# Cross-attention block: context rows laid out with their ones columns and loaded whole, and a new order on all five engines

## The reference, cut to what matters

```
n  = layernorm(x)
gi = concat([n, ctx, ctx])                 # q, k and v: q = n, k = v = ctx
ig, fg = gi @ igate_w.T + igate_b, gi @ fgate_w.T + fgate_b
cs = cumsum(log_sigmoid(fg))               # along the 256 rows, per head
log_D = tril(cs[s] - cs[t]) + ig[t];  m = max_t log_D;  D = exp(log_D - m)
C  = (q @ k.T / 8) * D
h  = (C / (max(|sum C|, exp(-m)) + 1e-6)) @ v
x  = x + headnorm(h) * out_w
z  = e4m3(layernorm(x) / s_in);  w = e4m3(ffn_kernel / s_k)
out = x + bf16(z @ w * s_in * s_k) + bias
```

## Time and profile before

| | |
|---|---|
| median of 3 runs | 1749.72 us (1747.93 to 1753.19) |
| span of the profiled execution | 1755.2 us |
| busy in it: PE, DVE | 1600.4 us (91%), 1550.3 us (88%) |
| ACT, POOL | 1284.9 us (73%), 1103.1 us (63%) |
| share of the chain that ended last | PE 61%, DVE 19%, issue 10%, DMA 7% |

### The profile page before, as it was taken

One profiled execution on the slowest core, in us unless ns is written; L12 is line 12 of the kernel. 1 busy time (PEld: TensorE's weight loads), 2 busy tenths in 40 slices (PEclk: granted clock), 3 DMA queues, 4 the chain that ended last, 5 costly groups with the idle time before them and its releaser, 6 DMA issues.

```text
span 1755.2 us, 88770 instructions
## 1 busy us (share of the span) xinstructions
PE 1600.4 (91%) x36224; PEld 1193.1 (68%) x36224; DVE 1550.3 (88%) x4161; ACT 1284.9 (73%) x3137; POOL 1103.1 (63%) x1040
## 2 busy tenths in 40 slices
PE   3779999999999998999999999999999999999985
PEld 1567776777667676777776777776777777777762
DVE  6679988999888899998998989999999999998884
ACT  3657777777777777777777777777778777777653
POOL 1056666666566666666666666666667666666774
PEclk9889999999999999999999999999999999999996
DMA  4748978888878788788888788888888888887542
GB/s 165 206 150 222 247 214 214 231 232 216 235 218 225 218 213 232 217 232 229 226 221 232 214 226 230 225 239 214 225 241 225 226 231 240 218 223 216 166 134 84
DMA packets 329911, 376.11 MB, mean 214 GB/s; under 512 B 17056, under 2 KB 214688, under 8 KB 329504
## 3 DMA queue, kind: packets, MB, share of 16 engines
q1 hardware_dynamic: 329504, 370.40, 76.8%
HBM read 303.22 MB, written 67.11 MB: 211 GB/s over the span
## 4 chain that ended last, share of the span: by engine, by line
PE 61%; DVE 19%; issue 10%; DMA 7%; ACT 2%; POOL 1%; DVEq 0%; POOLq 0%; ACTq 0%
PE work L509 10%; PE y L548 9%; PE qk L477 9%; PE turn L392 7%; PE turn L403 5%; DMA o_sb<-in_x 4%; DVE dec L913 4%; PE work L489 3%; PE arg L446 3%; DMA out<-o_sb 3%; DVE bn L967 3%; DVE o_sb L1007 3%; PE y L532 2%; PE y L546 2%; PE work L521 2%
## 5 line engine op out<-in xcount | busy, mean ns | idle before, releaser
L1150 POOL TENSOR_TENSOR x<-x,h_r 128x512 f32<-128x512 f32 x256 | 269.6, 1053 | 268.9 <-DVE x L959 154.6
L1163 POOL TENSOR_TENSOR x<-x,w_out 128x512 f32<-128x512 f32 x256 | 358.1, 1399 | 20.1
L1168 POOL TENSOR_TENSOR x<-x,o_sb 128x512 f32<-128x512 f32 x256 | 321.1, 1275 | 33.7 <-DMA o_sb<-in_x 33.0
L509 PEld LDWEIGHTS work<-c_first,dec 128*64 128x64 f32 x4096 | 265.3, 138 | 72.1 <-issue 70.4
L509 PE MATMUL work<-c_first,dec 128*64 128x65 f32 x4096 | 290.8, 224 | 13.2 <-issue 6.4
L509 PE MATMUL work<-c_sb,dec 128*64 128x65 f32 x4096 | 292.7, 224 | 5.7 <-issue 5.7
L509 PEld LDWEIGHTS work<-c_sb,dec 128*64 128x64 f32 x4096 | 265.3, 138 | 6.4 <-issue 6.1
L548 PE MATMUL y<-w_ffn,zq 128*128 128x512 bf16 x1024 | 266.4, 383 | 0.0
L477 PE MATMUL qk<-qT,kT 64*64 64x128 f32 (+1 forms) x8192 | 235.8, 251 | 32.6 <-DVE dec L913 24.9
L614 ACT ACTIVATE dec<-arg 128x384 f32<-128x384 f32 x512 | 243.6, 476 | 27.9 <-PE arg L458 26.8
L1007 DVE SCALAR_TENSOR_TENSOR o_sb<-y,s_out,x 128x512 f32<-128x512 f32 x256 | 190.5, 744 | 73.1 <-PE y L548 72.3
(11 more groups left out here) (122 smaller groups left out, 4680.7 us busy)
## 6 DMA issues: line engine op xcount, KB each, us to landing
x_sb<-in_x SPq DMA_DIRECT2D x128, 512.0 KB, 5.1
kT<-in_keys SPq DMA_DIRECT2D x128, 512.0 KB, 6.7
c_sb<-in_ctx SPq DMA_DIRECT2D x256, 256.0 KB, 5.7
o_sb<-in_x SPq DMA_DIRECT2D x128, 512.0 KB, 4.5
out<-o_sb SPq DMA_DIRECT2D x128, 512.0 KB, 3.3
c_first<-in_ctx SPq DMA_DIRECT2D x256, 128.0 KB, 5.4
w_ffn<-in_L_ffn_kernel SPq DMA_DIRECT2D x1, 512.0 KB, 10.2
w_out<-in_L_xattn_out_w SPq DMA_DIRECT2D x1, 256.0 KB, 11.6
```

Of the source, the lines that this page charges most:

```text
L509: last = mm(work_ps[rows, u, c * W:(c + 1) * W], heads_dec[:, slot * Q:(slot + 1) * Q], src, start=True, stop=True)
L1150: pl.tensor_tensor(h, h, h_r[:, t * NH:(t + 1) * NH].unsqueeze(2).broadcast_to([P, NH, DH]), ALU.mult).then_inc(h_normed[t].sem, 1)
L1163: pl.tensor_tensor(h, h, w_out[:, :], ALU.mult).then_inc(h_scaled[t].sem, 1)
L1168: pl.tensor_tensor(x1[:, b.k % 2, t, :], x1[:, b.k % 2, t, :], o_sb[:, b.k % 2, t, :], ALU.add).then_inc(x1_set[t].sem, 1)
```

## The change

The host stores the context rows with both columns of ones: 130 columns for each of the four chunks, 4160 bytes a partition for both tiles. `load_c` becomes one DMA of whole rows in place of two with 512-byte pieces, and `load_first` brings whole rows of 2080 bytes. The memsets of the ones go (one group on POOL, four on DVE). The rest is order: `slot` of SP, PE, ACT, DVE and POOL is written anew. The operations and their shapes are the same, and no wait is added or taken from a step, apart from the counts that the DMA and setup changes need. Lines without a change are mostly left out.

```diff
@@ -279,7 +279,7 @@
         N_FFN_W_SET = ROUNDING * C
-        N_POOL_SET, N_FIRST_SET, N_SCAN_SET, N_DVE_SET = 9, 15, 18, 29
+        N_POOL_SET, N_FIRST_SET, N_SCAN_SET, N_DVE_SET = 8, 11, 14, 25
         N_WIDE = ROUNDING * WIDE_PIECES
@@ -304,15 +304,14 @@
             def context(b):
-                return ctx[bass.ds(b.k, 1), :, :, :].rearrange("o p t (c e) -> p (o t) c e", c=C)
+                return ctx[bass.ds(b.k, 1), :, :, :, :].rearrange("o p t c e -> p (o t) c e")
 
...
                     sp.wait_ge(*summed[1].of(b - C_RING))
-                for t in range(T):
-                    sp.dma_start(values(b, t), context(b)[:, t, :, :]).then_inc(c_in[r], 16)
+                sp.dma_start(c_sb[:, r, :, :, :], context(b)).then_inc(c_in[r], 16)
 
@@ -330,7 +329,7 @@
                     rows = slice(t * Q, (t + 1) * Q)
-                    sp.dma_start(c_first[rows, r, t, :, 1:1 + U * DH], context(b)[rows, t, :, :]).then_inc(first_in[r], 16)
+                    sp.dma_start(c_first[rows, r, t, :, :], context(b)[rows, t, :, :]).then_inc(first_in[r], 16)
 
@@ -353,18 +352,18 @@
             def slot(m):
-                if live(m + 10):
-                    load_x(m + 10)
-                if live(m - 2):
-                    load_own(m - 2)
+                if live(m - 1):
+                    load_first(m - 1)
+                if live(m - 3):
+                    load_own(m - 3)
                 if live(m + 7):
...
                 if live(m + 1):
-                    load_first(m + 1)
-                if live(m + 3):
-                    load_c(m + 3)
-                if live(m - 3):
-                    store(m - 3)
+                    load_c(m + 1)
+                if live(m - 4):
+                    store(m - 4)
+                if live(m + 10):
+                    load_x(m + 10)
 
@@ -550,23 +549,12 @@
             def slot(m, wide_z):
-                if live(m + 3):
-                    arg(m + 3, 0)
-                if scans(m + 3):
-                    scan_turn(m + 3)
-                if live(m + 9):
-                    turn_round(m + 9, 1)
-                if live(m - 1):
-                    ffn(m - 1, 1, wide_z)
-                if live(m + 2):
-                    within(m + 2, 0)
-                if live(m + 3):
-                    arg(m + 3, 1)
-                    scores(m + 3, 0)
                 if live(m + 2):
                     across(m + 2)
-                if live(m + 9):
-                    gates(m + 9)
+                if live(m + 3):
+                    scores(m + 3, 0)
+                if scans(m + 4):
+                    scan_turn(m + 4)
                 if live(m + 3):
@@ -575,15 +563,28 @@
                     arg(m + 3, 3)
-                    scores(m + 3, 1)
                 if scans(m + 6):
                     scan_rows(m + 6)
+                if live(m + 3):
+                    scores(m + 3, 1)
+                if live(m):
+                    ffn(m, 0, wide_z)
                 if live(m + 10):
                     turn_round(m + 10, 0)
-                if live(m):
-                    ffn(m, 0, wide_z)
+                if live(m + 4):
+                    arg(m + 4, 0)
                 if live(m + 3):
                     states(m + 3)
+                if live(m):
+                    ffn(m, 1, wide_z)
+                if live(m + 10):
+                    turn_round(m + 10, 1)
+                if live(m + 3):
+                    within(m + 3, 0)
+                if live(m + 4):
+                    arg(m + 4, 1)
+                if live(m + 10):
+                    gates(m + 10)
 
@@ -748,58 +749,56 @@
             def slot(m):
-                if live(m - 2):
-                    quantise(m - 2)
-                if live(m + 1):
-                    decay(m + 1, 3)
+                if scans(m + 2):
+                    keep_facs(m + 2)
                 if scans(m + 4):
...
                     scan_relu(m + 4)
-                if scans(m + 2):
-                    scan_exps(m + 2)
+                    scan_exp(m + 4)
                 if live(m):
...
                     keep_turned(m + 8, 0)
-                if live(m):
-                    head_log(m)
                 if scans(m + 4):
-                    scan_exp(m + 4)
+                    scan_log(m + 4)
                 if live(m + 1):
...
                     x_logs(m + 10)
-                if scans(m + 4):
-                    scan_log(m + 4)
                 if live(m + 2):
                     decay(m + 2, 0)
-                if scans(m + 2):
-                    keep_facs(m + 2)
+                if live(m + 10):
+                    x_rstds(m + 10)
                 if live(m + 8):
                     keep_turned(m + 8, 1)
+                if scans(m + 3):
+                    scan_exps(m + 3)
+                if live(m + 1):
+                    keep_heads(m + 1)
+                if live(m):
+                    head_log(m)
                 if live(m + 9):
                     norm_apply(m + 9, 0)
-                if live(m + 1):
-                    keep_heads(m + 1)
-                if live(m + 9):
-                    norm_apply(m + 9, 1)
                 if live(m - 1):
                     m_logs(m - 1)
-                if live(m):
-                    head_rstd(m)
-                if live(m - 1):
                     m_rstds(m - 1)
...
                     decay(m + 2, 1)
+                if live(m):
+                    head_rstd(m)
+                if live(m + 8):
+                    keep_gates(m + 8)
                 if live(m - 1):
...
                     z_apply(m - 1, 1)
-                if live(m + 10):
-                    x_rstds(m + 10)
                 if live(m + 2):
                     decay(m + 2, 2)
-                if live(m + 8):
-                    keep_gates(m + 8)
+                if live(m - 1):
+                    quantise(m - 1)
+                if live(m + 9):
+                    norm_apply(m + 9, 1)
+                if live(m + 2):
+                    decay(m + 2, 3)
 
@@ -818,9 +817,6 @@
             setup(ve.memset(n_eps[:, :], EPS * N_SCALE))
-            for t in range(T):
-                for r in range(2):
-                    setup(ve.memset(c_first[t * Q:(t + 1) * Q, r, t, :, 0:U * W:U * W - 1], 1.0))
             setup(ve.memset(ln_qs[:, :], math.log(Q_SCALE)))
@@ -1058,58 +1054,57 @@
                     ffn_weights(m.k - (FIRST + 4))
+                if live(m + 9):
+                    norm_stats(m + 9, 0)
+                if live(m - 4) and wide_z:
+                    quantise_wide(m - 4)
+                if live(m - 4):
+                    finish(m - 4, 0)
                 if live(m - 1):
                     matrix(m - 1, 1)
+                if scans(m + 2):
+                    scan_sums(m + 2)
+                if scans(m + 1):
+                    scan_exponents(m + 1)
                 if live(m + 9):
                     norm_stats(m + 9, 1)
-                if live(m - 3):
-                    mix_stats(m - 3, 0)
                 if live(m - 4):
...
                 if live(m - 3):
+                    mix_stats(m - 3, 0)
+                if live(m + 8):
+                    norm_scale(m + 8)
+                if live(m - 3):
                     mix_stats(m - 3, 1)
-                if scans(m + 1):
-                    scan_max(m + 1)
-                if scans(m + 2):
-                    scan_sums(m + 2)
+                if live(m + 9):
+                    norm_moments(m + 9)
                 if live(m - 3):
...
                 if scans(m + 1):
-                    scan_exponents(m + 1)
-                if live(m + 9):
-                    norm_moments(m + 9)
+                    scan_rest(m + 1, 0)
+                if scans(m + 2):
+                    scan_a(m + 2)
                 if live(m - 3):
...
                     carried(m - 1)
-                if scans(m + 1):
-                    scan_rest(m + 1, 0)
                 if live(m - 2):
...
                 if live(m - 1):
+                    head_stats(m - 1, 0)
                     keep_heads(m - 1)
-                    head_stats(m - 1, 0)
-                    normaliser(m - 1)
                 if scans(m + 1):
                     scan_rest(m + 1, 1)
-                if live(m + 8):
-                    norm_scale(m + 8)
+                if scans(m + 2):
+                    scan_max(m + 2)
                 if live(m - 1):
+                    normaliser(m - 1)
+                    head_stats(m - 1, 1)
                     normaliser_clip(m - 1)
-                if live(m + 10):
-                    norm_stats(m + 10, 0)
-                if live(m - 1):
-                    head_stats(m - 1, 1)
-                if scans(m + 2):
-                    scan_a(m + 2)
-                if live(m - 3) and wide_z:
-                    quantise_wide(m - 3)
-                if live(m - 3):
-                    finish(m - 3, 0)
 
@@ -1117,9 +1112,6 @@
             pl = nc.gpsimd
```

(32 more changed lines are left out.)

## The result

The changed kernel is slower. Its median is 1778.99 us against 1749.89 us before; the ratio is 1.0155 with a 95% interval of 1.0122 to 1.0188. I had forecast 1720 us. The profiled execution grew less, from 1755.2 to 1775.1 us.

A forecast was written before the change was run, and what follows sets the result against it. PE was taken as the bound, losing 3.7 us of each 51.9 us group. A group was to fall to 48.2 + 1.4 + 1.1 = 50.7 us; over 29 groups -35, with the start -30, giving 1720 us, range 1688 to 1770.

The forecast's parts named there:

- The sum: Time per four batches: PE's work 48.2 us (four plain slots of 11.70, scan_rows, scan_turn) plus stops, 50.7 after the change.
- emptying and filling: PE's pipeline emptying and filling around stops, with small waits: 1.3 us a group before, left out of the sum after.
- issue: PE stopped inside a block with nothing to wait for: 1.6 us a group before, 1.4 after the change.
- What bounds the kernel, and the loss of 3.7 us a group: PE's 48.2 us of a 51.9 us group; loss: 1.6 issue stops, 0.8 waiting for DVE's matrix, 1.3 emptying and filling.
- Context loads: Fewer small DMA packets let PE's instructions arrive sooner: 0 to 0.8 us a group, taken as 0.2.
- PE order, the seams: Overlap of neighbouring PE blocks, 16 seams new: 0 us, with a bound of 0.2 us a slot either way.
- DVE order: Scan steps spread over two slots, DVE contending with POOL's SBUF reads: PE loses 0.3 to 1.9 us a group, taken as 1.1.
- DVE's free time: DVE's slack beside PE, 11.7 - 10.5 = 1.2 us a slot, said to cover head_centre 1's loss of about 0.5.
- ACT order, my slower rival: ACT's unbroken run keep_heads to z_apply, 4.28 us against PE's 4.23, costs 0; rival: it bounds, 1768 us, chance 0.20.
- The lock moving in full: Rival: second scan_rest and some head_centre wait out POOL's SBUF reads, 1.9 us a group or more; 1747 us, chance 0.13.
- SP order: SP's new queue of loads and stores: load_own's wait for the store still holds by 1 us, so cost 0.
- Start and end: Memsets gone before the first matmul, -0.5 us; norm_apply 1 later in the ramp, +5 (0 to +8); end 0.

The follow-up runs named there:

- e12: Kernel before with the new loads, and POOL's four large steps replaced by memsets of about equal length that read nothing: 1710.1 us, ratio 0.9792.
- e1: Kernel before with the load part of the change alone, every order as before: 1727.71 us, ratio 0.9924.
- e5: Kernel before, old loads, with POOL's four large steps replaced by memsets that read nothing: 1732.21 us, ratio 0.9896.
- e10: Kernel before with the new loads and both scan_rest done by POOL in place of DVE: 1712.08 us, ratio 0.9777; repeated 1709.43 us, 0.9783.
- e2: Changed kernel with the loads and memsets of before, so the new order alone: 1777.87 us, ratio 1.0179 to the kernel before.
- e3: Changed kernel with POOL's four large steps replaced by memsets that read nothing: 1734.7 us, ratio 0.9938 to the kernel before.
- e6: Changed kernel with one operand of scan_sums and of scan_exponents put in PSUM: 1758.79 us, ratio 1.0059 to the kernel before.
- e11: Changed kernel with both scan_rest moved from DVE to POOL, between weigh_keys and head_norm: 1746.68 us, ratio 0.9995 to the kernel before.
- e9: Changed kernel with the edits of e6 and e8 together: 1758.57 us, ratio 1.0063 to the kernel before.
- e8: Changed kernel with the second scan_rest directly after the first, ahead of mix_scale: 1796.19 us, ratio 1.0269 to the kernel before.
- e15: The kernel of e3 with SP's order of before: 1721.68 us, ratio 0.9849 to the kernel before.
- e17: The kernel of e12 with SP's new order: 1726.67 us, ratio 0.9878 to the kernel before.
- e14: Changed kernel with SP's order of before, everything else as changed: 1770.31 us, ratio 1.0136 to the kernel before.
- e7: Kernel before with the new loads and the first scan_rest moved on DVE to directly after mix_moments: 1726.58 us, ratio 0.9863; repeated 1721.97 us, 0.9855.
- e16: The kernel of e10 with scan_exponents moved directly after scan_max: 1716.58 us, ratio 0.9822 to the kernel before.

## Why the prediction was wrong, point by point

- **The sum.** This is the first step that failed. The prediction had 51.9 us a group before, 1.3 of it for "emptying and filling", and 50.7 after, "with 1.3 for emptying and filling that I leave out because it goes with the stops". Its terms for stops and DVE alone went from 2.4 to 2.5; the gain of 1.2 us was the term left out. It does not go with the stops. From before to e12, stops and waits fall from 2.5 to 1.0 us a group, and the remainder stays at 49.3 and 49.2; in the changed kernel it is 49.1, where the sum has 48.2. The plain slot of 11.70 us is the shortest one: 24 plain slots of before without any stop or wait take 11.92 on average. With the term kept, the sum would have forecast a group 0.1 us longer.
- **The sum against the trace.** A group was to take 48.2 + 1.4 (issue) + 1.1 (DVE) = 50.7 us. It takes 49.1 + 1.1 + 2.1 = 52.3: 0.9 us more in the remainder, 1.0 more in waits with a releaser, most of them for DVE, 0.3 less in stops. Over 29 groups the 1.6 us are 46 of the 50 us between the forecast of the profiled execution, 1725, and its 1775.1.
- **What bounds the kernel, and the loss of 3.7 us a group.** Right in kind for two of its three parts. The part "issue" is confirmed by e1, in which it falls to a third; the part of DVE by e5, in which the waits with a releaser fall from 19.7 to 6.9 us, and by e10. The third part is the one above.
- **Context loads, "0 to 0.8 us a group. I take 0.2".** The mechanism was right and the size wrong: 0.76% or 13 us with the loads alone, 0.4 us a group by the time and 0.8 to 1.1 by PE's stops. I had said that no row ties the stops to the DMA load, which was true, and took that for evidence of a small effect. In the changed kernel little of it is left: with SP's new order the stops are 22.7 us in 1000 with the old loads (e2) and 22.9 with the new ones.
- **PE order, the seams.** Within its bound. The shortest distance from a batch's y to the next batch's in the changed kernel's timeline is 11.59 us, against 11.70, and the remainder of a group is 0.2 us smaller.
- **DVE order.** This is the second step that failed, 2.1 us a group in place of 1.1. "12.3 in a slot where PE needs 11.7 to 12.1" counted scan_exponents at 0.4 us and scan_sums at its old length. I weighed the lock for scan_rest and head_centre alone, though the rule that I had just named says scan_sums too. Moved by half a slot, these two fell beside POOL's residual, in 37 of 38 cases. The three that I did lay out came as said: the first rest 0.68 us, the second 1.74, head_centre 1 up to 1.26. The lock is 3.6 us a group: 1.2 in head_centre, which I let DVE's free time cover whole, 1.1 in the second rest, and 1.3 in the two steps that I had not priced. With that the free time was gone: DVE at 1625.0 us is busy for 92%. Without the lock (e3) the waits with a releaser fall to 0.2 us a group.
- **The free time itself.** I let one allowance, 1.2 us a slot, cover head_centre's lock, the lateness of the scan slots and the waits for y. By DVE's busy time, 0.8 us a group less gave 0.5 us (e6), 1.8 less gave 0.9 (e11) and 0.5 (e9), 3.2 less gave 1.2 (e3). So time on DVE is neither free below a threshold nor full above one, and what it is worth depends on its place: e8 took a little off DVE and lost 1.1%.
- **ACT order, my slower rival.** It did not come. PE never waited for z_apply in the stretch, and for a decay 4.1 us. The forecast of a slower kernel by that road would have had the right sign for the wrong reason. The run is as tight as I said: DVE waited for m_rstds in 38 of 76 slots, 0.3 us each.
- **The lock moving in full, "1747 us, no change".** The right mechanism, sized too small by the two steps left out, and with the same 1.3 us missing from its sum.
- **SP order, priced at 0.** Wrong where it can be seen: 0.9% in e15 and in e17. It is not measurable in the changed kernel (e14).
- **Start and end.** y starts at 116.7 us, against 117.0 before, which looks like nothing and is two things. The new loads alone bring it to 112.3 us, and SP's new order takes that back. The +5 us for norm_apply did not come: with all new orders but SP's, y starts at 111.3 us (e14).
- **The range**, 1688 to 1770, failed at its upper end by 9 us. It should have held the case in which every DVE instruction with two SBUF operands meets POOL, since the trace of before gave the price for it.

## What to carry to other kernels

A remainder that no row explains belongs in the sum of the kernel after as in that of the kernel before; to let it go is a forecast of its own and needs a row. When an order is laid out anew, list every instruction that shares a resource with another engine, and place all of them, not only those that suffered in the old trace: a step that hardly met its rival has a short mean that says nothing of its new place. Moving work off the engine that loses (here the rests to POOL) held, while moving it in time (e7, e16) moved the collision to another step or kept it. And test the parts of a change alone: here one part was a gain of 0.8% and hid behind a loss of 2.3%.

## What the runs showed of the hardware that I had not expected

- DVE's instructions with two SBUF operands wait for a POOL instruction that reads SBUF, up to its end, and do not wait for memsets of the same length: scan_exponents 1.156 against 0.403 us, scan_sums 1.200 against 0.674. This holds for a 32-partition scan as for a 128-partition subtraction.
- With one of the two operands in PSUM the same steps run at 0.67 and 0.40 us beside a reading POOL (e6).
- PE's stops without any releaser end 1.0 to 1.8 us after the end of a 16 KB packet of instructions: all 33 before, all 30 in the changed kernel, between 400 and 1400 us.
- In the old order these stops are 30.8 and 27.3 us in 1000 (before, e5) with 1536 packets of 512 bytes a batch, and 7.3 to 15.0 us in seven profiles with 256 larger ones in their place. In the new order the same loads left 9.4 to 35.7 us (e14 and e3, leaving out profiles with some matmul records missing), and 22.7 us came with the old ones (e2); why is open.
